# Reordering an attention block's instruction streams: k's weights split ahead of the fourth output weight, tile 4 masked and split in another order, the tail's transposes spread

## The reference

```python
h = _layernorm(x) * (1 + ca) + sa
x = x + ga * attention(h)          # 32 heads of 128, 8 k/v heads, rope, causal softmax, then @ wo
h = _layernorm(x) * (1 + cb) + sb
x = x + gb * ffn(h)                # h @ W.T + b, plus one of four low-rank terms chosen by a router
```

## Time and profile before

| what | us |
|---|---|
| median of 3 runs | 1114.86 (1112.5 to 1119.03) |
| the profiled execution, its own time | 1113.62 |
| its span | 1111.8 |
| TensorE busy | 1055.0 (95%) |
| VectorE busy | 775.7 (70%) |
| ScalarE busy | 635.4 (57%) |
| GpSimd busy | 521.9 (47%) |

### The profile page before, as it was taken

How to read it: one execution, slowest core, us unless ns; L and a number is a source line. 1 busy time by engine, 2 the same in 40 slices (tenths; PEclk the granted TensorE clock), 3 DMA queues, 4 the chain that set the end, 5 groups by cost and what they waited for, 6 DMA issues and landing times.

```text
span 1111.8 us, 16527 instructions
## 1 busy us (share of the span) xinstructions
PE 1055.0 (95%) x5416; PEld 867.1 (78%) x5416; DVE 775.7 (70%) x1834; ACT 635.4 (57%) x1298; POOL 521.9 (47%) x506
## 2 busy tenths in 40 slices
PE   6999999998999989999999999999999999998897
PEld 3668878887878878887878878887878878887775
DVE  4668866588558866588557865678647865678576
ACT  5547754477337654477437754477436753477433
POOL 2535553365425654365425643365425652455244
PEclk8999999999999999999999999999999999999999
DMA  6562323133302233033202233033212223024001
GB/s 212 152 216 67 103 79 76 39 95 95 78 18 68 85 96 76 34 98 97 71 25 67 86 95 77 12 109 99 57 49 67 77 86 95 3 97 130 10 20 57
DMA packets 99004, 88.22 MB, mean 79 GB/s; under 512 B 39460, under 2 KB 84644, under 8 KB 98792
## 3 DMA queue, kind: packets, MB, share of 16 engines
q1 hardware_dynamic: 98920, 87.17, 26.6%
HBM read 59.88 MB, written 27.26 MB: 78 GB/s over the span
## 4 chain that ended last, share of the span: by engine, by line
PE 56%; DVE 14%; ACT 12%; POOL 7%; issue 6%; DMA 4%; SPq 1%; POOLq 0%; DVEq 0%; ACTq 0%
PE accumulators L649 14%; PE accumulators L664 13%; PE accumulators L679 13%; PE scores L609 6%; PE transposed L622 6%; DVE p_large L1172 3%; POOL qc L1539 3%; ACT pb_hi L907 2%; ACT pa_hi L913 2%; DVE turned L1196 2%; POOL qr L1535 2%; DVE pb_lo L1184 2%; ACT qr L932 2%; PE scores L864 2%; ACT qr L931 2%
## 5 line engine op out<-in xcount | busy, mean ns | idle before, releaser
L907 ACT ACTIVATE pb_hi<-transposed 128x512 fp32r<-128x512 f32 (+3 forms) x256 | 117.5, 511 | 211.7 <-PE transposed L622 211.5
L1526 POOL TENSOR_SCALAR p_large<-p_large,rowinv 128x640 f32<-128x640 f32 (+3 forms) x128 | 125.1, 978 | 229.0 <-DVE rowinv L1177 229.0
L1535 POOL TENSOR_TENSOR qr<-qr,trig 128x512 f32<-128x512 f32 x80 | 104.4, 1305 | 221.1 <-ACT qr L932 221.0
L1184 DVE TENSOR_TENSOR pb_lo<-transposed,pb_hi 128x512 fp32r<-128x512 f32 (+3 forms) x256 | 138.9, 584 | 94.0 <-ACT pb_hi L907 93.6
L899 ACT ACTIVATE p_large<-p_large,negmax 128x640 f32<-128x640 f32 (+3 forms) x128 | 126.3, 986 | 87.6 <-DVE negmax L1172 87.5
L609 PE MATMUL scores<-k_hi,q_hi 128*128 128x512 f32 (+2 forms) x384 | 139.3, 363 | 1.7 <-DVE negmax L1172 1.7
L1172 DVE CUSTOM_DVE_ANT_0 p_large<-scores,mask 128x640 f32<-128x640 f32 (+3 forms) x128 | 129.4, 1011 | 4.0 <-PE scores L609 3.7
L609 PE MATMUL scores<-k_hi,q_lo 128*128 128x512 f32 (+2 forms) x384 | 131.4, 342 | 0.0
L609 PE MATMUL scores<-k_lo,q_hi 128*128 128x512 f32 (+2 forms) x384 | 131.1, 341 | 0.0
L1526 POOL TENSOR_SCALAR p_small<-p_small,rowinv 128x128 f32<-128x128 f32 (+3 forms) x128 | 97.2, 775 | 71.6 <-DVE rowinv L1177 71.6
L622 PE MATMUL transposed<-ident,p_large 128*128 128x128 f32 x832 | 113.9, 275 | 12.3 <-DVE pb_lo L1184 6.1
(11 more groups left out here) (165 smaller groups left out, 2225.9 us busy)
## 6 DMA issues: line engine op xcount, KB each, us to landing
p_rows<-turned SPq DMA_DIRECT2D x32, 640.0 KB, 2.9
pa_lo<-p_rows SPq DMA_DIRECT2D x128, 160.0 KB, 3.1
stage<-in_L_attn_wq_dram SPq DMA_DIRECT2D x32, 256.0 KB, 2.8
stage<-in_L_attn_wo_dram SPq DMA_DIRECT2D x32, 256.0 KB, 2.7
v_rows<-vt SPq DMA_DIRECT2D x32, 128.0 KB, 2.2
v_lo<-v_rows SPq DMA_DIRECT2D x32, 128.0 KB, 3.1
y<-in_L_wmod_dram SPq DMA_DIRECT2D x4, 512.0 KB, 5.7
stage<-in_L_attn_wk_dram SPq DMA_DIRECT2D x8, 256.0 KB, 2.7
```

The source lines that it names most:

```text
L907: nc.scalar.activation(pt_of(i, part, True), src, ACT.Copy).then_inc(t_hi, 1)
L1184: nc.vector.tensor_tensor(pt_of(i, part, False), src, f32(pt_of(i, part, True)), ALU.subtract).then_inc(t_lo, 1)
L1526: nc.gpsimd.tensor_scalar(row(i), row(i), rowinv[:, i:i + 1], 1.0, ALU.mult, ALU.mult).then_inc(s_norm, 1)
L1535: nc.gpsimd.tensor_tensor(qr[:, s, :], qr[:, s, :], trig[:, 1, half * HALF:(half + 1) * HALF], ALU.mult).then_inc(r_sin, 1)
```

## The change

Five edits of order; no operation is added or removed, and no tile changes size.

1. k's weights take the place of the fourth output weight in the load sequence, and are split before it on ScalarE and VectorE. The last group, which has no next k, is untouched.
2. `parts(4)` is reversed: tile 4's single block 4 is transposed and split first, then blocks 0 to 3.
3. In heads 1 to 3, `front` on VectorE masks tile 4 before the subtraction of the previous head's output, not after it.
4. In head 0, `back` on VectorE does `inverse` of tile 7 and the additions to `y` before `early_lo`, not after it.
5. The tail is rearranged on TensorE, ScalarE and VectorE: W0 stands between the scores of tiles 4 and 5, W1 before tile 4's transposes, W2 and W3 after the transposes of tile 5 and the scores of tile 7; A and B come after `weighted(3, 0)` and tile 6's transposes.

```diff
 def parts(i):
-    return [range(0, min(i, 3) + 1)] + ([range(4, i + 1)] if i >= 4 else [])
+    halves = [range(0, min(i, 3) + 1)] + ([range(4, i + 1)] if i >= 4 else [])
+    return halves[::-1] if i == 4 else halves
...
-            if part == 0:
+            if js[0] == 0:
...
-        W_LATE = [("q", 0), ("wo", 3), ("k", 0), ("v", 0)]
+        W_LATE = [("q", 0), ("k", 0), ("wo", 3), ("v", 0)]
...
                 if g + 1 < GROUPS:
                     load(("q", 0), at, 1)
+                    load(("k", 0), at, 1)
                     load(("wo", 3), at)
-                    load(("k", 0), at, 1)
...
 # TensorE, tail
             scores(3, 4, G7)
-            scores(3, 5, G7)
             pe.wait_ge(f_in, 16)
             weight_transposes(0)
+            scores(3, 5, G7)
             weight_transposes(1)
             transposes(3, 4, G7)
             scores(3, 6, G7)
+            transposes(3, 5, G7)
             weight_transposes(2)
-            transposes(3, 5, G7)
+            scores(3, 7, G7)
             weight_transposes(3)
-            scores(3, 7, G7)
+            weighted(3, 0, G7)
+            transposes(3, 6, G7)
             pe.wait_ge(f_low_in, 16 * 3)
...
-            weighted(3, 0, G7)
-            transposes(3, 6, G7)
             project_out(0, G7, 0)
...
 # ScalarE, back()                      (VectorE, back(): the same two lines with split_lo)
                 if last:
+                    split_hi(("k", 0), at, 1)
                     split_hi(("wo", 3), at)
-                    split_hi(("k", 0), at, 1)
...
 # VectorE, front()
                 turn(h, at, 0, 1, 2)
+                if h:
+                    masked(h, 4, at)
                 if h or not at.first:
                     output_lo(hb, 1, at, ahead)
-                masked(h, 4, at)
+                if not h:
+                    masked(h, 4, at)
                 turn(h, at, 3)
...
 # VectorE, back()
-                early_lo(h, at)
+                if h:
+                    early_lo(h, at)
                 inverse(h, 7, at)
                 if h == 2:
                     split_lo(("wo", 2), at)
                 fill(h, 5, at, slice(0, -1))
+                if not h:
+                    early_lo(h, at)
...
 # VectorE, tail
+            weight_lo(("W", 0), 1, fw_hi[:, 0, :], fw_lo[:, 0, :])
             inverse(3, 4, G7)
             masked(3, 5, G7)
             inverse(3, 5, G7)
+            transposed_lo(3, 4, G7)
+            weight_lo(("W", 1), 2, fw_hi[:, 1, :], fw_lo[:, 1, :])
+            masked(3, 6, G7)
             split_lo(("wo", 3), G7)
...
+            masked(3, 7, G7)
+            early_lo(3, G7)
             weight_lo(("W", 2), 3, fw_hi[:, 2, :], fw_lo[:, 2, :])
...
             output_lo(3, 0, G7)
             transposed_lo(3, 6, G7)
+            weight_lo(("A", 0), 5)
+            weight_lo(("B", 0), 6, fb_hi, fb_lo, MAX_R)
             add_output(0, G7, 0)
```

More of the change, by code:

```diff
@@ L174, in tail @@
         self.step("s", (3, 4), g)
+        self.job(("W", 0, 0), g)
         self.step("s", (3, 5), g)
-        self.job(("W", 0, 0), g)
         self.job(("W", 1, 0), g)
@@ L179, in tail @@
         self.step("s", (3, 6), g)
+        self.banks(3, 5, g)
         self.job(("W", 2, 0), g)
-        self.banks(3, 5, g)
+        self.step("s", (3, 7), g)
         self.job(("W", 3, 0), g)
-        self.step("s", (3, 7), g)
+        self.job(("pva", 3, 0), g)
+        self.banks(3, 6, g)
         self.job(("A", 0, 0), g)
         self.job(("B", 0, 0), g)
-        self.job(("pva", 3, 0), g)
-        self.banks(3, 6, g)
         self.job(("wo", 0, 0), g)
@@ L439, in w_number @@
             elif what == ("wo", 3):
-                base = len(W_FIRST) + len(W_GROUP) + (2 if at.g + ahead < GROUPS - 1 else 1) + W_PER * (at.g + ahead)
+                base = len(W_FIRST) + len(W_GROUP) + (3 if at.g + ahead < GROUPS - 1 else 1) + W_PER * (at.g + ahead)
             elif at.g + ahead == 0:
@@ L1077, in _ @@
             exp(3, 4, G7)
+            weight_hi(("W", 0), fw_hi[:, 0, :])
             exp(3, 5, G7)
+            transposed_hi(3, 4, G7)
+            weight_hi(("W", 1), fw_hi[:, 1, :])
             split_hi(("wo", 3), G7)
-            weight_hi(("W", 0), fw_hi[:, 0, :])
-            weight_hi(("W", 1), fw_hi[:, 1, :])
-            transposed_hi(3, 4, G7)
+            exp(3, 6, G7)
+            transposed_hi(3, 5, G7)
+            early_hi(3, G7)
             weight_hi(("W", 2), fw_hi[:, 2, :])
-            transposed_hi(3, 5, G7)
-            exp(3, 6, G7)
+            exp(3, 7, G7)
             weight_hi(("W", 3), fw_hi[:, 3, :])
+            output_hi(3, 0, G7)
+            transposed_hi(3, 6, G7)
             weight_hi(("A", 0), vt[:, 0:KC * AG], cols=KC * AG)
-            early_hi(3, G7)
-            exp(3, 7, G7)
             weight_hi(("B", 0), fb_hi, MAX_R)
-            transposed_hi(3, 6, G7)
-            output_hi(3, 0, G7)
             def second_norm(t):
@@ L1351, in back @@
                 if last:
+                    split_lo(("k", 0), at, 1)
                     split_lo(("wo", 3), at)
-                    split_lo(("k", 0), at, 1)
                 inverse(h, 6, at)
@@ L1427, in _ @@
             inverse(3, 5, G7)
+            transposed_lo(3, 4, G7)
+            weight_lo(("W", 1), 2, fw_hi[:, 1, :], fw_lo[:, 1, :])
+            masked(3, 6, G7)
             split_lo(("wo", 3), G7)
[L1429 to L1432, removed]
+            inverse(3, 6, G7)
+            transposed_lo(3, 5, G7)
+            masked(3, 7, G7)
+            early_lo(3, G7)
             weight_lo(("W", 2), 3, fw_hi[:, 2, :], fw_lo[:, 2, :])
-            transposed_lo(3, 5, G7)
-            inverse(3, 6, G7)
+            inverse(3, 7, G7)
             weight_lo(("W", 3), 4, fw_hi[:, 3, :], fw_lo[:, 3, :])
[L1437 to L1441, removed]
             output_lo(3, 0, G7)
             transposed_lo(3, 6, G7)
+            weight_lo(("A", 0), 5)
+            weight_lo(("B", 0), 6, fb_hi, fb_lo, MAX_R)
             add_output(0, G7, 0)
```

## The result

| what | before | after |
|---|---|---|
| median | 1117.64 us (1112.50 to 1119.04, 6 runs) | 1125.26 us (1123.81 to 1128.76, 6 runs) |
| ratio, 95% interval | | 1.0079 (1.0053 to 1.0106) |
| the profiled execution: own time, span | 1113.62, 1111.8 | 1124.94, 1123.2 |

The changed kernel is slower by 0.8%, about 9 us, where 1118.0 with a range up to 1123 was forecast. The median of the three runs shown beforehand was itself low: over six runs the kernel before has 1117.64, and over the 88 runs taken beside the experiments medians of 1117.0 to 1119.1.

The account below looks back on a forecast made before the run. TensorE, busy 1055.0 of 1111.8 us, was taken as the bound. Terms 0 - 1.0 + 6.9 + 0.8 - 2.2 + 0.8 - 2.5 = +2.8 gave 1116.4, plus 1.2 for the median: 1118, range 1109.5 to 1123.

Parts of the forecast that it names:

- The steady terms: Order effects in heads and tail: edit 2 -1.0, edit 3 +6.9 and +0.8, edit 4 -2.2, edit 5 +0.8 us.
- 6.9 + 0.8: Masking tile 4 first delays the chain to its transposes: +6.9 us in heads 1 and 2, +0.8 in head 3.
- against 0.28: Head 0, fourth weight row's addition to y: starts 0.28 us sooner in each of eight groups, -2.2 in all.
- against 1.0: Tile 5's transposes: their waits go, but the next fixed point keeps nearly all of it; -1.0 us in all.
- the fixed point: Next start timed by another engine, where TensorE's gained time is lost; in head 3 the first v job.
- against +0.8: Tail: tile 4's transposes come later, and the first output projection starts about 0.8 us later.
- edit 1's term: k's split first: k starts 1.68 us earlier in seven places, but v starts as before; 0, bounds 0 and -11.8.
- The clock's term of -2.5: Two of seven groups had clock falls behind the k wait; these go with that wait: -2.5 us, bounds 0 and -3.3.
- The rival, falls in front of v at 1.7 each: Clock falls at the 1.9 us idle before v, two or three times, +4.2 us on average: 1122; chance 0.22.
- the +2.8: Sum of all terms for the whole kernel, +2.8 us, added to the profiled execution's 1113.62 to give 1116.4.
- Tile 5's 0.35: Rival: TensorE keeps the 0.35 us gained at tile 5's transposes in 32 heads, -11.2 us: 1107.5; chance 0.13.
- the masking was not free: Denies the rival that tile 4's scores are ready when VectorE arrives, so the 6.9 us falls away: 1110.8; chance 0.15.

Follow-up runs that it names:

- the move: Kernel before with k's swap_halves ahead of early_hi and tile 7's exponential, k's times_cos ahead of early_lo, in head 3: 1118.02 us, ratio 0.9987.
- each half alone: Against the kernel before: edit 1 by itself, ratio 1.0029, and the move by itself, 0.9987; edit 1 with the move took 1108.03 us, 0.9902.

## Why the prediction was wrong

**The steady terms were right.** Edit 3 measured 7.8 against 6.9 + 0.8. Edit 4 gave 0.23 a group against 0.28. Edit 2 gave some 2 in all against 1.0, since in its own trace head 3, where the v job was taken for the fixed point, kept 0.15 a group too. Edit 5 measured +0.9 in the mean of the traces against +0.8. In the changed kernel they are 4.6 + 0.9 = +5.5; 4.5 + 0.8 was forecast.

**The step that failed is edit 1's term, "The term is 0; its bounds are 0 and -11.8".** The working behind it was right: v starts when ScalarE's list lets it, and the idle 0.23 became 1.7 to 2.2. But the bounds had no side of loss. v's load stands at the head of that same list on ScalarE, with tile 7's exponential and k's `swap_halves` behind it, and whatever makes the load late goes into the group in full. In the changed kernel's traces two late loads cost 3.2 each (49.7 less 46.5), half by the landing and half by the clock behind a 3.5 us wait: 6.4 us. The runs put edit 1 at the same 6.4 there, with an interval of 3 to 10; how many of the unprofiled runs had late loads is open.

**The clock's term of -2.5 was half right.** The falls behind k did go: the two traces of the changed kernel have none there. They are worth 1.05 to 1.1 each, a little less than the 1.25 worked out, since more of the 1.7 was slack than the 0.4 assumed. The rival, falls in front of v at 1.7 each, had the mechanism and the price right: 48.2 in place of 46.6 in the groups of edit 1's traces. It was priced with equal waits of 1.9; that two of them would be 3.5 was not seen. Over 18 traces, by the longest idle stretch of TensorE in the group:

| idle stretch | groups | with a low clock behind it |
|---|---|---|
| k, 2.0 us | 42 | 15 |
| k, 2.3 us | 21 | 9 |
| v, 1.7 to 2.5 us | 35 | 10 |
| v, 3.4 to 4.0 us | 7 | 7 |
| none over 1.3 us (with the move) | 21 | 0 |

The counts differ between kernels with the same stretch (behind a k wait of 2.3, none of seven in the change without edit 1 and five of seven with edits 2 and 4 alone), so they are no rate for a single kernel.

The Trainium skill (TensorE: Matmul & The Clock Gate, part 1) says that activity is what releases the throttle, so that an idle stretch is a reason for a fall wherever it stands. By that rule the falls should follow the wait from k to v, and the traces agree: 10 of 35 there, and all seven of the longest.

**The base was low.** The sum was made on a profiled execution of 1113.62 that lacked the start-up's low clock, and on a median of three runs, 1114.86, which is 2.8 below that of six. Added to 1117.64, the +2.8 would have given 1120.4 and left 4.8 open, less than the late loads of the traces.

**The other rivals.** Tile 5's 0.35 was not kept (edit 2 alone gave 0.02 to 0.15 a head), and the masking was not free. Both had a small chance, rightly.

Worked out from these, the change is 4.6 steady, 0.9 for the tail, 6.4 for the late loads with their falls and 0.8 for falls behind v without a late load (one in ten such groups of the two traces, 1.6 each, in five groups), less 2.7 for the falls behind k that went (15 in 42 groups, 1.1 each, in seven groups). That is 10.0, inside the interval of the ratio, 5.9 to 11.8 us. Without late loads, and with falls behind v in 10 of 35 groups, the same sum is 6.0, which the interval does not rule out either. What is shown is that edit 1 costs something beside the others, and that edit 3 is the steady loss; how edit 1's part divides is read from two profiles alone.

## What to carry to other kernels

When an edit shortens one wait and the next one takes its place, ask what queue times the second, and move that as well: here each half alone gave nothing or less, and both gave 1%. A move that only shifts idle time is not free, because the clock can fall behind it and because a chain without slack passes on every late transfer. Put a subtraction or a copy into time in which its engine would wait for scores anyway; moved out of it, most of its length comes into the chain (0.44 of 0.60 here). Take the base from more than three executions, and look whether the profiled one has the same clock as the others.

## What was not expected of the hardware

- Loads of data land late where they meet a packet of an instruction queue. Where a packet of queue q8, 0.02 MB and 1.1 to 1.9 us long, started 1.0 to 2.0 us after the issue of v's 256 KB load, the load landed 1.5 to 2 us late (8 of 8, against none of 118). This is a coincidence in time seen in traces; no run moved a packet by itself.
- TensorE's granted clock fell to 0.5 behind idle stretches of 2.0 us, in 15 of 42 cases of the same stretch in the same place. So one profile doesn't tell what such a wait costs. It needs a count over several.
- The same fall cost 1.05 to 1.1 us behind k, where the next wait, 0.2 to 0.3 in front of v, took up a part of it, and 1.6 to 1.7 behind v, where nothing did. With the move on the kernel before, no wait is left in front of the first v job, and there a fall behind k cost 1.6 too (48.2 in place of 46.6, twice).
